# Bf16 pair one-hots, a fused block search and an index fill ahead of the stores in a graph kernel

## The chip, the cores and the metric

The kernel runs on one core of a Trainium2 chip. The metric is the time of one execution on the device in microseconds (us), as the median of several executions.

Five engines run their own instruction streams beside each other and meet at semaphores. TensorE (PE) multiplies matrices into PSUM and loads the weights for it (PEld). VectorE (DVE) and ScalarE (ACT) do elementwise work and reductions. GpSimd (POOL) here issues the indirect DMAs, which gather rows by an index or scatter them. SyncE (SP) issues the plain DMAs.

## The reference

A graph of 6250 nodes with 256 features and 106250 edges (50000 random pairs in both directions and one loop per node, sorted by `dst`) goes through two blocks, each behind a layer normalization and a ReLU, and each added to its input.

```python
h = jnp.maximum(_layernorm(x, axis=-1), 0.0)
# block 0: two hops over the graph
support = h @ weight
h1 = spmm(src, dst, edge_weight, support)      # sum over edges: h1[src] += w * support[dst]
h2 = spmm(src, dst, edge_weight, h1)
x = x + relu(hop_w[0] * h1 + hop_w[1] * h2 + h)
h = jnp.maximum(_layernorm(x, axis=-1), 0.0)
# block 1: neighbour sum and a net of four layers
agg = segment_sum(h[src], dst)
h = (1.0 + eps) * h + agg
h = elu(bn(h @ W1 + b1)); h = elu(bn(h @ W2 + b2)); h = elu(bn(h @ W3 + b3))
x = x + h @ W4 + b4
```

The hops add into `src`, while the edges come sorted by `dst`. So the kernel sorts the edges by `src` itself before it can add them up window by window.

## The kernel before

The kernel is written engine by engine (one function per engine, from line 549 on). The order on each engine is the order of the code, and the engines wait for one another by `wait_ge` on named semaphores. It goes through these stages: normalization, support and bin counts; a rank of every edge in its window; the block search and the sort loop; the sorted edges back into SBUF; hop 1; hop 2 with the second normalization beside it; the neighbour sum with the first layer beside it; the rest of the net.

**Block search.** The edges lie in 832 columns of 128 (`TILES`), which form 16 bins (`BINS`) of 52 columns. A sorted block holds 8 edges of one window (`SLOT`). Each bin has 7 registers of 128 blocks (`REG`). For each bin, register and partition the kernel must find where the block goes in DRAM: it compares 50 start numbers (`NA`) with the block's number, multiplies by the jump at each start and adds up. Before, the starts and the jumps both stand in PSUM (banks 2 and 3, 4 and 5), and the two halves of the bins go one after another: a comparison, a product and a reduction over 8 x 7 x 50 = 2800 elements each (lines 1299 to 1307). `chain` makes the next instruction wait for the one it wraps.

**Sort loop.** The 832 columns go in 64 batches of 13 (`BATCH`, `BATCHES`). In batch k, VectorE makes a one-hot of the slot (13 x 56 elements, line 1323, semaphore `slot_hot`), a one-hot of the partition (13 x 128, line 1328, `part_hot`) and the product of the slot one-hot with the packed edge (line 1332, `load_v`). ScalarE makes the product with the edge weight in 13 activations of 56 columns (line 917, `load_w`). TensorE multiplies the partition one-hot with both products (line 1838, `moved_mm`) and adds up four batches, a bin, in PSUM. All buffers of the loop are double: VectorE's slot one-hot of batch k waits for ScalarE's batch k-2, and the partition one-hot of VectorE and the activations of ScalarE wait for TensorE's batch k-2. After every fourth batch ScalarE copies the bin out of PSUM (`take_bin`, line 908) into one of three buffers, whose earlier bin must have been stored. GpSimd then scatters the bin's 7 registers to DRAM (line 754, `bin_stored`). When all bins are stored, SyncE reads the sorted edges back.

**Hops.** Each hop has 108 groups of 8 columns. Per group ScalarE copies eight index columns into a ring of three (`fill_hop`, line 938, `hop_idx`), GpSimd gathers 8 x 128 rows (`gather`, line 787), VectorE builds one-hots, TensorE multiplies, and VectorE adds. Hop 2 gathers the sums of hop 1, which SyncE stores to `table_hop2` chunk by chunk (`h1_stored`). GpSimd waits for all 13 stores before its first gather of hop 2. Before, ScalarE waits for them too, ahead of its first index copy of hop 2 (lines 967 to 968). Its normalizations in hop 2 write over the sums of hop 1, the first of them in group 16.

**Names.** `w1_all` and `w1_hi_all` are weight buffers that serve as scratch in the sort (`place_i`, `slot_f`). `sum_b` becomes the sums of hop 1 and is scratch before. `work` holds the loop's buffers. `both` gives each such buffer an f32 name, an fp32r name and a bf16 name (`_h`) over the same bytes. `edge_buf` and all that is cut from it (`part_f`, `packed`, `w_all`, the bin numbers) are f32; `iota` is bf16.

Of the kernel before, what the change touches and what calls it, by code (L numbers as in the profile page):

```python
# [43 lines left out]
P = 128  # L44
# [112 lines left out]
def gnn(nc, x, src_t, dst_t, dst_g, w_t, wg, logits, eps, W1, b1, g1, be1, W2, b2, g2, be2,  # L157
        W3, b3, g3, be3, W4, b4, out):
    with ExitStack() as ctx:
# [30 lines left out]
        sum_b, sum_r, sum_h = both("sum_b", DH * ROWS)  # L190
        edge_buf = sb("edge_buf", [P, 4 * TILES + STILES])
        work, work_r, work_h = both("work", 8 * CW)
        w1_all, w1_r, _ = both("w1", K1 * H1)
        w1_sb = w1_all[:, :].rearrange("p (k m) -> p k m", k=K1)
        w4_sb = w1_all[:, :].rearrange("p (k m) -> p k m", k=K4)
        w1_hi_all, w1_hi_sb, w1_hi_h = both("w1_hi", K1 * H1)
# [94 lines left out]
        assert at[0] <= TILES  # L291

        place_i = w1_hi_all[:, 0:TILES].bitcast(I32)
        slot_f = w1_all[:, 0:TILES]
        part_f = dst_loc
        scratch = [sum_b[:, n * TILES:(n + 1) * TILES].bitcast(I32) for n in range(4)]
        at_or_above = sum_b[:, 4 * TILES:4 * TILES + HB * REG * NA].rearrange("p (g r a) -> p g r a", g=HB, a=NA)
        to_block_f = sum_b[:, 4 * TILES + 2 * HB * REG * NA:4 * TILES + 2 * HB * REG * NA + BINS * REG]
        at = [0]
        hot_part = place(2 * BATCH * P).rearrange("p (s t w) -> p s t w", s=2, t=BATCH)  # L300
        hot_slot = place(2 * BATCH * BCOLS).rearrange("p (s t w) -> p s t w", s=2, t=BATCH)
        load = place(2 * BATCH * BCOLS * 2).rearrange("p (s t w v) -> p s t w v", s=2, t=BATCH, v=2)
        ev_bin = place(3 * BCOLS * 2).rearrange("p (s w) -> p s w", s=3)
        to_block = place(BINS * REG).bitcast(I32)
# [77 lines left out]
        def bank(b, n):  # L382

            return ps[:, b, 0:n]
# [44 lines left out]
        spread_mm = sem("spread_mm")  # L429
        rank_mm = sem("rank_mm")  # L430
        rank_picked = sem("rank_picked")
        blocks_placed = sem("blocks_placed")
        places_made = sem("places_made")
        sums_zeroed = sem("sums_zeroed")
# [426 lines left out]
        def _(act):  # L861
# [42 lines left out]
            def take_bin(g):  # L904
# [2 lines left out]
                    act.wait_ge(bin_stored[g % 3], 16 * REG * (g // 3))  # L907
                act.copy(ev_bin[:, g % 3, :], bank(4 + g % 2, 2 * BCOLS)).then_inc(bin_out, 1)

            act.wait_ge(edges_in, 64)  # L910
            act.wait_ge(zeros_stored, 16 * GT)
            for k in range(BATCHES):
# [34 lines left out]
            def hop2_step(i, k, first, last):  # L947
                fill_hop(1, i, k, first)
                c, q = chunk_at(i, k, 5)
                if c is not None:  # L950
                    root(1, c, q, CT)
                c, q = chunk_at(i, k, 7)
                if c is not None:
                    norm(1, c, q, CT)
                c, q = chunk_at(i, k, 8)
                if c is not None:
                    to_cols(c, q, CT)
# [6 lines left out]

            with act.If(near):
                over_hop(act, lambda i, k, first, last: fill_hop(0, i, k, first))
                act.wait_ge(h1_kept, CHUNKS)
                act.wait_ge(h1_stored, 16 * CHUNKS)
                over_hop(act, hop2_step)
                for c in (FULL - 1, FULL):  # L970
                    root(1, c, c % 2, tiles_of(c))
                for c in (FULL - 1, FULL):
                    norm(1, c, c % 2, tiles_of(c))
                for c in (FULL - 1, FULL):
                    to_cols(c, c % 2, tiles_of(c))
# [141 lines left out]
        def _(dve):  # L1117
# [177 lines left out]
            chain(dve.tensor_scalar(scratch[0], place_i, 3, 127, ALU.logical_shift_right, ALU.bitwise_and))  # L1295
            chain(dve.tensor_tensor(scratch[3], scratch[1], scratch[2], ALU.bitwise_or))
            dve.tensor_copy(part_f, scratch[0])
            chain(dve.tensor_copy(slot_f, scratch[3]))
            for half in range(2):
                at_ = [P, HB, REG, NA]  # L1300
                blocks_ = block_no[:, :].unsqueeze(1).unsqueeze(3).to_broadcast(at_)
                start_, jump_ = [bank(b + half, HB * NA).rearrange("p (g a) -> p g a", a=NA).unsqueeze(2).to_broadcast(at_)
                                 for b in (2, 4)]
                chain(dve.tensor_tensor(at_or_above, start_, blocks_, ALU.is_le))
                chain(dve.tensor_tensor(at_or_above, at_or_above, jump_, ALU.mult))
                to = to_block_f[:, half * HB * REG:(half + 1) * HB * REG].rearrange("p (g r) -> p g r", r=REG)
                chain(dve.tensor_reduce(to, at_or_above, AX_X, ALU.add))
            for half in range(2):
# [8 lines left out]
            for k in range(BATCHES):  # L1317
                par = k % 2
                cols = slice(k * BATCH, (k + 1) * BATCH)
                if k >= 2:  # L1320
                    dve.wait_ge(load_w, k - 1)
                at_ = [P, BATCH, BCOLS]
                dve.tensor_tensor(hot_slot[:, par], iota[:, 0:BCOLS].unsqueeze(1).to_broadcast(at_),  # L1323
                                  slot_f[:, cols].unsqueeze(2).to_broadcast(at_), ALU.is_equal).then_inc(slot_hot, 1)
                if k >= 2:
                    dve.wait_ge(moved_mm, k - 1)
                at_ = [P, BATCH, P]
                dve.tensor_tensor(hot_part[:, par], iota[:, 0:P].unsqueeze(1).to_broadcast(at_),
                                  part_f[:, cols].unsqueeze(2).to_broadcast(at_), ALU.is_equal).then_inc(part_hot, 1)
                dve.wait_ge(slot_hot, k + 1)  # L1330
                at_ = [P, BATCH, BCOLS]
                dve.tensor_tensor(load[:, par, :, :, 0], hot_slot[:, par],
                                  packed[:, cols].unsqueeze(2).to_broadcast(at_), ALU.mult).then_inc(load_v, 1)
# [734 lines left out]
```

## Time and profile before

| | |
|---|---|
| median of 3 executions | 4485.47 us (4483.37 to 4486.48) |
| the profiled execution's own time | 4485.46 us |
| its span, first to last instruction | 4483.8 us |
| mean granted TensorE clock | 0.929 |
| busy: TensorE | 3297.6 us (74%) |
| busy: VectorE | 1898.1 us (42%) |
| busy: ScalarE | 796.5 us (18%) |
| busy: GpSimd | 2702.0 us (60%) |

The shares are means over stages with different limits. What is said of one stage must be read from the timeline of that stage. A timeline row gives the start in us from the span's start, the length, the engine and line, what it writes and reads, the number of instructions merged into it, and in brackets the idle time of the engine ahead of it with what ended it. Ends of matmuls are modelled. The line numbers are those of the kernel before.

### The profile page before, as it was taken

How to read it: one execution, taken by the hardware profiler on the slowest of the kernel's cores; microseconds unless marked ns; L12 is line 12 of the kernel's file. 1: busy time of each engine (PE TensorE's matmuls, PEld its weight loads, DVE VectorE, ACT ScalarE, POOL GpSimd, SP SyncE). 2: the span in 40 equal slices, each digit the busy share in tenths (PEclk: the TensorE clock that was granted, in tenths of full speed). 3: DMA queues.
4: the chain of work that ended last, by engine and by line, in shares of the span. 5: the costliest groups of instructions: out<-in, count | busy, mean ns of one | idle time of the engine just before them, and what ended most of it. 6: DMA issues, size and time to landing. Idle time of an engine off the chain costs nothing. (4 is left out here: it accounts for less than half of the span.)

```text
span 4483.8 us, 50632 instructions
## 1 busy us (share of the span) xinstructions
PE 3297.6 (74%) x15959; PEld 2720.9 (61%) x15959; DVE 1898.1 (42%) x4482; ACT 796.5 (18%) x1968; POOL 2702.0 (60%) x2708
## 2 busy tenths in 40 slices
PE   6779577777777767777777774566666665998998
PEld 5278555555555555566655654555555554887887
DVE  7889333333333323333333332222222223556766
ACT  4079100000000000000000000000000001545656
POOL 1088677777777767777777775777777775001000
PEclk9899899999999999999999996888888887999999
DMA  4000233333333343333333344433333333223323
GB/s 141 1 3 6 76 108 109 113 109 109 109 110 112 108 95 109 109 109 112 109 109 109 113 106 120 130 105 105 105 104 104 105 105 92 89 97 125 97 70 115
DMA packets 205561, 443.80 MB, mean 99 GB/s; under 512 B 47053, under 2 KB 121089, under 8 KB 205289
## 3 DMA queue, kind: packets, MB, share of 16 engines
q0 software_dynamic: 126464, 336.63, 26.2%
q1 hardware_dynamic: 78933, 105.26, 7.1%
q8 instruction: 69, 1.13, 0.1%
q14 instruction: 95, 0.78, 0.1%
HBM read 382.22 MB, written 59.49 MB: 99 GB/s over the span
## 5 line engine op out<-in xcount | busy, mean ns | idle before, releaser
L1871 PE MATMUL ps<-work 128*128 128x256 f32 x6912 | 1622.4, 388 | 589.6 <-DMA work<-table_hop,idx 589.6
L787 POOL DMA_INDIRECT work<-table_hop,idx x1728 | 1662.3, 962 | 556.7 <-issue 522.7
L1871 PEld LDWEIGHTS ps<-work 128*128 128x128 f32 x6912 | 1293.2, 192 | 916.9 <-DMA work<-table_hop,idx 491.9
L832 POOL DMA_INDIRECT work<-table_gin,idx x832 | 791.5, 951 | 283.9 <-issue 228.8
L1946 PE MATMUL ps<-work 128*128 128x128 f32 x3328 | 569.5, 342 | 413.9 <-DMA work<-table_gin,idx 382.9
L1946 PEld LDWEIGHTS ps<-work 128*128 128x128 f32 x3328 | 524.7, 248 | 483.6 <-DMA work<-table_gin,idx 314.6
L1409 DVE TENSOR_SCALAR work<-iota,w_hi,edge_buf 128x256 f32<-128x256 bf16 x1728 | 581.4, 408 | 18.4 <-issue 17.3
L938 ACT COPY idx<-w 128x8 int32 (+1 forms) x216 | 42.1, 197 | 1953.9 <-PE ps L1871 1913.3
L1522 DVE TENSOR_TENSOR sum_b<-sum_b,ps 128x256 f32 x104 | 43.9, 422 | 801.0 <-PE ps L1946 801.0
L1421 DVE TENSOR_TENSOR sum_b<-sum_b,ps 128x512 f32 x108 | 74.2, 687 | 721.6 <-PE ps L1871 721.6
L1421 DVE TENSOR_TENSOR big<-big,ps 128x512 f32 x108 | 74.2, 687 | 697.8 <-PE ps L1871 697.8
L1903 PE MATMUL ps<-sum_b_r,work_r 128*128 128x482 f32 (+1 forms) x832 | 318.9, 383 | 35.2 <-DVE sum_b_r L1643 17.9
L1904 PE MATMUL ps<-sum_b_r,work_r 128*128 128x482 f32 (+1 forms) x832 | 318.3, 383 | 0.0
L1905 PE MATMUL ps<-sum_b_r,work_r 128*128 128x482 f32 (+1 forms) x832 | 318.1, 382 | 0.0
L1838 PE MATMUL ps<-work 128*128 128x112 f32 x1664 | 204.4, 281 | 64.9 <-ACT work L917 59.1
L1838 PEld LDWEIGHTS ps<-work 128*128 128x128 f32 x1664 | 195.2, 196 | 74.3 <-issue 74.3
L917 ACT ACTIVATE work<-work,edge_buf 128x56 f32<-128x56 f32 x832 | 200.2, 332 | 151.0 <-DVE work L1323 145.9
L754 POOL DMA_INDIRECT sorted_edges<-work x112 | 197.4, 1762 | 46.8 <-issue 33.2
L819 POOL TENSOR_TENSOR work_r<-work,work_r 128x512 fp32r<-128x512 f32 (+1 forms) x12 | 23.5, 1971 | 326.0 <-DVE work_r L1366 326.0
L1903 PEld LDWEIGHTS ps<-sum_b_r,work_r 128*128 128x128 f32 x832 | 157.3, 189 | 63.0 <-issue 35.6
L985 ACT CAST idx<-edge_buf 128x8 int32 (+1 forms) x104 | 20.2, 198 | 944.5 <-PE ps L1946 944.5
L1509 DVE TENSOR_SCALAR work<-iota,edge_buf 128x128 f32<-128x128 bf16 x832 | 176.2, 299 | 2.0 <-ACT sum_b L944 2.0
(225 smaller groups left out, 2639.7 us busy)
## 6 DMA issues: line engine op xcount, KB each, us to landing
work<-table_hop,idx POOLq DMA_INDIRECT x1728
z_dram<-sum_b SPq DMA_DIRECT2D x24, 964.0 KB, 4.1
sum_b<-z_dram SPq DMA_DIRECT2D x24, 964.0 KB, 5.2
work<-table_gin,idx POOLq DMA_INDIRECT x832
big<-x SPq DMA_DIRECT2D x12, 512.0 KB, 5.9
table_hop<-work SPq DMA_DIRECT2D x12, 512.0 KB, 2.9
table_hop<-sum_b SPq DMA_DIRECT2D x12, 512.0 KB, 3.4
x_dram<-big SPq DMA_DIRECT2D x12, 512.0 KB, 3.4
```

What stands on the lines that cost most here:

```text
L754: pool.indirect_dma_start(sorted_dram, bass.IndirectOffsetOnAxis(to_block[:, g * REG + r:g * REG + r + 1], 0), ev_bin[:, g % 3, r * 2 * SL ...
L787: pool.indirect_dma_start(hop_rows[:, par, t, :], None, table[n], bass.IndirectOffsetOnAxis(idx[:, k % HR, t:t + 1], 0)).then_inc(rows_in[ ...
L832: pool.indirect_dma_start(rows[:, par, t, :], None, table[2], bass.IndirectOffsetOnAxis(idx[:, q, t:t + 1], 0)).then_inc(rows_in[par][half ...
L917: last = act.activation(load[:, k % 2, t, :, 1], hot_slot[:, k % 2, t, :], ACT.Copy, scale=w_all[:, k * BATCH + t:k * BATCH + t + 1])
L1409: last = dve.tensor_scalar(hot[:, k % 2, t, :], iota[:, :], loc_sorted[:, at_], w_sorted[:, at_], ALU.is_equal, ALU.mult)
L1509: last = dve.tensor_scalar(onehot[:, q % 2, t, :], iota[:, 0:WIN], dst_loc[:, bass.ds(g * GT + t, 1)], None, ALU.is_equal)
L1838: mm = pe.matmul(bank(4 + g % 2, 2 * BCOLS), hot_part[:, k % 2, t, :], load[:, k % 2, t].rearrange("p w v -> p (w v)"), start=(r == 0 and ...
L1871: mm = pe.matmul(ps[:, HWIN * par + b, 0:D], hot[:, par, t, b * P:(b + 1) * P], hop_rows[:, par, t, :], start=(t == 0), stop=(t == GT - 1))
L1903: pe.matmul(to[:, 0:n], hi, a[:, 0, 0:n], start=start, stop=False)
L1904: pe.matmul(to[:, 0:n], hi, a[:, 1, 0:n], start=False, stop=False)
L1905: return pe.matmul(to[:, 0:n], lo, a[:, 0, 0:n], start=False, stop=stop)
L1946: mm = pe.matmul(ps[:, 2 * par + a, 0:WIN], rows[:, par, t, a * P:(a + 1) * P], onehot[:, par, t, :], start=(t == 0), stop=(t == GT - 1))
```

## The change

The slot number of an edge was an f32 number per column (`slot_f`). It is now a bf16 number that is written twice side by side (`slot_twice`), and the slot one-hot `hot_slot` is bf16 and made over pairs: its innermost dimension is two neighbouring columns, which meet the two copies of the slot number. ScalarE's and VectorE's products read the bf16 one-hot and still write f32. The partition one-hot is unchanged.

In the block search, ScalarE copies both start tables from PSUM to SBUF (`starts_of`, new semaphore `starts_kept`) as soon as the ranks are picked. VectorE then runs one fused operation per half and register (compare with the register's block number, times the jump), 7 of 400 elements a half, in place of the comparison and the product of 2800. The reduction stays.

In hop 2, ScalarE's wait for the stores of hop 1 moves from the first index copy to the first normalization.

```diff
@@ -190,7 +190,7 @@
         sum_b, sum_r, sum_h = both("sum_b", DH * ROWS)
         edge_buf = sb("edge_buf", [P, 4 * TILES + STILES])
         work, work_r, work_h = both("work", 8 * CW)
-        w1_all, w1_r, _ = both("w1", K1 * H1)
+        w1_all, w1_r, w1_h = both("w1", K1 * H1)
         w1_sb = w1_all[:, :].rearrange("p (k m) -> p k m", k=K1)
         w4_sb = w1_all[:, :].rearrange("p (k m) -> p k m", k=K4)
         w1_hi_all, w1_hi_sb, w1_hi_h = both("w1_hi", K1 * H1)
@@ -291,14 +291,18 @@
         assert at[0] <= TILES
 
         place_i = w1_hi_all[:, 0:TILES].bitcast(I32)
-        slot_f = w1_all[:, 0:TILES]
+        slot_twice = w1_h[:, 0:2 * TILES].rearrange("p (t u) -> p t u", u=2)
         part_f = dst_loc
         scratch = [sum_b[:, n * TILES:(n + 1) * TILES].bitcast(I32) for n in range(4)]
         at_or_above = sum_b[:, 4 * TILES:4 * TILES + HB * REG * NA].rearrange("p (g r a) -> p g r a", g=HB, a=NA)
         to_block_f = sum_b[:, 4 * TILES + 2 * HB * REG * NA:4 * TILES + 2 * HB * REG * NA + BINS * REG]
+        at = [4 * TILES + 2 * HB * REG * NA + BINS * REG]
+        starts_of = sum_b[:, at[0]:at[0] + BINS * NA].rearrange("p (g a) -> p g a", a=NA)
+        assert at[0] + BINS * NA <= DH * ROWS
         at = [0]
         hot_part = place(2 * BATCH * P).rearrange("p (s t w) -> p s t w", s=2, t=BATCH)
-        hot_slot = place(2 * BATCH * BCOLS).rearrange("p (s t w) -> p s t w", s=2, t=BATCH)
+        hot_slot = work_h[:, 2 * at[0]:2 * at[0] + 2 * BATCH * BCOLS].rearrange("p (s t w) -> p s t w", s=2, t=BATCH)
+        place(2 * BATCH * BCOLS)
         load = place(2 * BATCH * BCOLS * 2).rearrange("p (s t w v) -> p s t w v", s=2, t=BATCH, v=2)
         ev_bin = place(3 * BCOLS * 2).rearrange("p (s w) -> p s w", s=3)
         to_block = place(BINS * REG).bitcast(I32)
@@ -429,6 +433,7 @@
         spread_mm = sem("spread_mm")
         rank_mm = sem("rank_mm")
         rank_picked = sem("rank_picked")
+        starts_kept = sem("starts_kept")
         blocks_placed = sem("blocks_placed")
         places_made = sem("places_made")
         sums_zeroed = sem("sums_zeroed")
@@ -907,6 +912,11 @@
                     act.wait_ge(bin_stored[g % 3], 16 * REG * (g // 3))
                 act.copy(ev_bin[:, g % 3, :], bank(4 + g % 2, 2 * BCOLS)).then_inc(bin_out, 1)
 
+            act.wait_ge(rank_picked, 2 * BT)
+            act.wait_ge(spread_mm, 4)
+            act.copy(starts_of.rearrange("p (h g) a -> p h (g a)", h=2), ps[:, 2:4, 0:HB * NA]).then_inc(starts_kept, 1)
+
+
             act.wait_ge(edges_in, 64)
             act.wait_ge(zeros_stored, 16 * GT)
             for k in range(BATCHES):
@@ -950,6 +960,9 @@
                 if c is not None:
                     root(1, c, q, CT)
                 c, q = chunk_at(i, k, 7)
+                if first and c is not None:
+                    act.wait_ge(h1_kept, CHUNKS)
+                    act.wait_ge(h1_stored, 16 * CHUNKS)
                 if c is not None:
                     norm(1, c, q, CT)
                 c, q = chunk_at(i, k, 8)
@@ -964,8 +977,6 @@
 
             with act.If(near):
                 over_hop(act, lambda i, k, first, last: fill_hop(0, i, k, first))
-                act.wait_ge(h1_kept, CHUNKS)
-                act.wait_ge(h1_stored, 16 * CHUNKS)
                 over_hop(act, hop2_step)
                 for c in (FULL - 1, FULL):
                     root(1, c, c % 2, tiles_of(c))
@@ -1295,14 +1306,16 @@
             chain(dve.tensor_scalar(scratch[0], place_i, 3, 127, ALU.logical_shift_right, ALU.bitwise_and))
             chain(dve.tensor_tensor(scratch[3], scratch[1], scratch[2], ALU.bitwise_or))
             dve.tensor_copy(part_f, scratch[0])
-            chain(dve.tensor_copy(slot_f, scratch[3]))
+            chain(dve.tensor_copy(slot_twice, scratch[3].unsqueeze(2).to_broadcast([P, TILES, 2])))
             for half in range(2):
-                at_ = [P, HB, REG, NA]
-                blocks_ = block_no[:, :].unsqueeze(1).unsqueeze(3).to_broadcast(at_)
-                start_, jump_ = [bank(b + half, HB * NA).rearrange("p (g a) -> p g a", a=NA).unsqueeze(2).to_broadcast(at_)
-                                 for b in (2, 4)]
-                chain(dve.tensor_tensor(at_or_above, start_, blocks_, ALU.is_le))
-                chain(dve.tensor_tensor(at_or_above, at_or_above, jump_, ALU.mult))
+                start_ = starts_of[:, half * HB:(half + 1) * HB, :]
+                jump_ = bank(4 + half, HB * NA).rearrange("p (g a) -> p g a", a=NA)
+                if half == 0:
+                    dve.wait_ge(starts_kept, 1)
+                for r in range(REG):
+                    last = dve.scalar_tensor_tensor(out=at_or_above[:, :, r, :], in0=start_, scalar=block_no[:, r:r + 1],
+                                                    in1=jump_, op0=ALU.is_le, op1=ALU.mult)
+                chain(last)
                 to = to_block_f[:, half * HB * REG:(half + 1) * HB * REG].rearrange("p (g r) -> p g r", r=REG)
                 chain(dve.tensor_reduce(to, at_or_above, AX_X, ALU.add))
             for half in range(2):
@@ -1319,9 +1332,10 @@
                 cols = slice(k * BATCH, (k + 1) * BATCH)
                 if k >= 2:
                     dve.wait_ge(load_w, k - 1)
-                at_ = [P, BATCH, BCOLS]
-                dve.tensor_tensor(hot_slot[:, par], iota[:, 0:BCOLS].unsqueeze(1).to_broadcast(at_),
-                                  slot_f[:, cols].unsqueeze(2).to_broadcast(at_), ALU.is_equal).then_inc(slot_hot, 1)
+                at_ = [P, BATCH, BCOLS // 2, 2]
+                columns = iota[:, 0:BCOLS].rearrange("p (w u) -> p w u", u=2).unsqueeze(1).to_broadcast(at_)
+                dve.tensor_tensor(hot_slot[:, par].rearrange("p t (w u) -> p t w u", u=2), columns,
+                                  slot_twice[:, cols, :].unsqueeze(2).to_broadcast(at_), ALU.is_equal).then_inc(slot_hot, 1)
                 if k >= 2:
                     dve.wait_ge(moved_mm, k - 1)
                 at_ = [P, BATCH, P]
```

On VectorE, around the block search, the last cast, the first half and the first batch stand like this before (`sum_b` holds the search's scratch, `w` the slot numbers, `work` the one-hots; `dve_small` is the semaphore of `chain`):

```order
L1298 CAST w<-sum_b 128x832
L1304 TENSOR_TENSOR sum_b<-ps,block_no 128x2800 [waits dve_small]
L1305 TENSOR_TENSOR sum_b<-sum_b,ps 128x2800 [waits dve_small]
L1307 TENSOR_REDUCE sum_b<-sum_b 128x56 [waits dve_small]
...
L1311 TENSOR_TENSOR work<-sum_b,block_no 128x56 [waits dve_small]
...
L1314 MEMSET done 128x1
L1323 TENSOR_TENSOR work<-iota,w 128x728
L1328 TENSOR_TENSOR work<-iota,edge_buf 128x1664
L1332 TENSOR_TENSOR work<-work,edge_buf 128x728 [waits slot_hot]
```

and like this after the change:

```order
L1309 CAST w_h<-sum_b 128x1664
L1316 SCALAR_TENSOR_TENSOR sum_b<-sum_b,block_no,ps 128x8x50 [waits starts_kept,dve_small]
L1316 SCALAR_TENSOR_TENSOR sum_b<-sum_b,block_no,ps 128x8x50 x6
L1320 TENSOR_REDUCE sum_b<-sum_b 128x56 [waits dve_small]
...
L1324 TENSOR_TENSOR work<-sum_b,block_no 128x56 [waits dve_small]
...
L1327 MEMSET done 128x1
L1337 TENSOR_TENSOR work_h<-iota,w_h 128x728
L1342 TENSOR_TENSOR work<-iota,edge_buf 128x1664
L1346 TENSOR_TENSOR work<-work_h,edge_buf 128x728 [waits slot_hot]
```

Two operations over 2800 elements became seven over 8 x 50, the first of which waits for ScalarE's copy. The cast writes 1664 elements in place of 832. The loop has the same three instructions in the same order, the first of them now into bf16.

On ScalarE, where hop 2 begins, the index copies (`idx<-w`) and the first normalization (`lsd<-lve`, `sum_b<-big,lnm,lrs`) stand like this before:

```order
L938 COPY idx<-w 128x8 [waits sorted_ready,hop_mm] x18
L938 COPY idx<-w 128x8 [waits hop_mm,sorted_ready,h1_stored,h1_kept]
L938 COPY idx<-w 128x8 [waits sorted_ready,hop_mm] x14
L868 ACTIVATE lsd<-lve 128x4 [waits ln1_var]
L938 COPY idx<-w 128x8 [waits sorted_ready,hop_mm] x2
L876 ACTIVATE sum_b<-big,lnm,lrs 128x256 [waits ln1_coef]
```

and after:

```order
L948 COPY idx<-w 128x8 [waits sorted_ready,hop_mm] x33
L873 ACTIVATE lsd<-lve 128x4 [waits ln1_var]
L948 COPY idx<-w 128x8 [waits sorted_ready,hop_mm] x2
L881 ACTIVATE sum_b<-big,lnm,lrs 128x256 [waits ln1_coef,h1_stored,h1_kept]
L881 ACTIVATE sum_b<-big,lnm,lrs 128x256 x3
L948 COPY idx<-w 128x8 [waits sorted_ready,hop_mm]
```

The first 18 copies of the first piece are the last of hop 1. The waits for `h1_stored` and `h1_kept` moved from the first copy of hop 2 to the first normalization, 16 groups on.

## Rows read from the trace of the kernel before

**Rows 1.** Busy time by stretch of the sort loop; then clock, DMA share, GB/s

```profile
217.60:299.13 81.53, 55.82 (x442) 53.45 (x442) 65.83 (x59) 56.90 (x239) 67.53 (x12) 0.86 0.01 2
299.13:462.92 163.79, 148.57 (x1222) 141.77 (x1222) 155.72 (x135) 145.29 (x609) 133.24 (x95) 0.99 0.03 6
```

**Rows 2.** Timeline, VectorE, search and first batch (start, us, what, idle before)

```profile
194.24 0.59 DVE L1292 TENSOR_SCALAR w_hi<-w 128x832 int32<-128x832 f32 x1
...
198.07 0.58 DVE L1298 CAST w<-sum_b 128x832 f32<-128x832 int32 x1
198.69 3.08 DVE L1304 TENSOR_TENSOR sum_b<-ps,block_no 128x2800 f32<-128x2800 f32 x1
201.80 3.07 DVE L1305 TENSOR_TENSOR sum_b<-sum_b,ps 128x2800 f32<-128x2800 f32 x1
...
217.60 0.91 DVE L1323 TENSOR_TENSOR work<-iota,w 128x728 f32<-128x728 bf16 x1
...
218.43 1.88 DVE L1328 TENSOR_TENSOR work<-iota,edge_buf 128x1664 f32<-128x1664 bf16 x1
220.23 0.91 DVE L1332 TENSOR_TENSOR work<-work,edge_buf 128x728 f32<-128x728 f32 x1
221.05 0.91 DVE L1323 TENSOR_TENSOR work<-iota,w 128x728 f32<-128x728 bf16 x1
```

**Rows 3.** Groups by line of VectorE, shapes apart (busy us, mean ns, idle before)

```profile
L1638 DVE SCALAR_TENSOR_TENSOR edge_buf<-edge_buf 128x482 f32<-128x482 f32 x144 | 94.6, 657 | 55.0 <-PE ps L1905 38.9 <-ACT edge_buf L1036 16.1
...
L1170 DVE TENSOR_TENSOR sum_b_h<-iota,edge_buf 128x784 bf16<-128x784 bf16 x32 | 29.4, 967 | 0.0
```

**Rows 4.** Timeline, ScalarE, two batches of the loop and its end

```profile
248.76 3.13 ACT L917 ACTIVATE work<-work,edge_buf 128x56 f32<-128x56 f32 x13 [0.33 <-DVE work L1323]
251.79 0.23 ACT L908 COPY work<-ps 128x112 f32<-128x112 f32 x1
252.21 3.13 ACT L917 ACTIVATE work<-work,edge_buf 128x56 f32<-128x56 f32 x13 [0.19 <-DVE work L1323]
...
462.92 0.25 ACT L908 COPY work<-ps 128x112 f32<-128x112 f32 x1 [3.31 <-PE ps L1838]
481.82 1.71 ACT L928 COPY edge_buf<-ps 128x432 f32<-128x432 f32 x2 [18.64 <-PE ps L1847]
```

**Rows 5.** Timeline, TensorE, one batch and the last

```profile
255.49 3.13 PE L1838 MATMUL ps<-work 128*128 128x112 f32 x26 [0.22 <-ACT work L917]
...
459.76 3.13 PE L1838 MATMUL ps<-work 128*128 128x112 f32 x26 [0.32 <-ACT work L917]
```

**Rows 6.** Waits of the loop (us in total, times, longest us)

```profile
ACT work L908 <- DMA sorted_edges<-work: 16.3, 1, 16.3
...
DVE work L1323 <- ACT work L917: 13.2, 1, 13.2
DVE work L1328 <- PE ps L1838: 6.7, 2, 4.2
```

**Rows 7.** Timeline, GpSimd, scatters of the sorted blocks

```profile
239.10 47.87 POOL L754 DMA_INDIRECT sorted_edges<-work  x1 [10.80 <-ACT work L908]
287.27 0.97 POOL L754 DMA_INDIRECT sorted_edges<-work  x1 [0.31 <-issue]
...
308.98 1.49 POOL L754 DMA_INDIRECT sorted_edges<-work  x1 [0.30 <-issue]
```

**Rows 8.** Timeline, VectorE, beside those scatters

```profile
285.01 0.91 DVE L1332 TENSOR_TENSOR work<-work,edge_buf 128x728 f32<-128x728 f32 x1
...
309.55 0.91 DVE L1332 TENSOR_TENSOR work<-work,edge_buf 128x728 f32<-128x728 f32 x1
```

**Rows 9.** Timeline, ScalarE and GpSimd, hop 1 to hop 2

```profile
1595.98 0.39 ACT L938 COPY idx<-w 128x8 int32<-128x8 int32 x3 [39.90 <-DMA table_hop<-sum_b]
1597.01 1.19 POOL L787 DMA_INDIRECT work<-table_hop,idx  x1 [16.48 <-ACT idx L938]
```


## The prediction

> **What bounds the kernel now.** I read the page first for the shares, then the busy time by stretch, then the timeline of each engine inside the sort, the waits of that stretch, and last the timeline where hop 1 passes into hop 2. The change touches three places: the block search, the loop of 64 batches that moves the edges into their slots, and the hand-over between the hops. Everything behind the first gather of hop 1 is the same program and only starts earlier, so I price the three places and shift the rest.
>
> In the loop VectorE is the busiest engine in both stretches, 65.83 of 81.53 us and 155.72 of 163.79 us [rows 1]. In the timeline it runs one batch after another without a gap: the slot one-hot (L1323) starts at 217.60, the partition one-hot (L1328) 0.83 us later, the product (L1332) 1.80 us after that, and the next batch's slot one-hot 0.82 us after that [rows 2]. That is 3.45 us a batch and 221 us for 64. From 217.60 to the end of TensorE's last batch at 459.76 + 3.13 = 462.89 [rows 5] are 245.3 us. The difference is 6.7 us of VectorE waiting for TensorE, 13.2 us of VectorE waiting for ScalarE [rows 6], and a tail of about 4 us in which TensorE finishes. The other engines are close behind. ScalarE starts its bin copy 3.03 us after the first of its 13 activations [rows 4], and TensorE's batch takes 3.13 us [rows 5]. So the question of the prediction is where the loop stops following VectorE.
>
> **Block search.** Before, each half runs a comparison and a product of 2800 elements and a reduction of as many. The first one starts at 198.69, the first batch at 217.60 [rows 2]: 18.9 us with VectorE alone at work. The product starts 3.11 us behind the comparison, and the three of a half are 3 x 3.11 = 9.3 us. After, the two tensor operations of a half become seven fused ones of 400 elements. The nearest row is the same operation at 482 elements, 657 ns [rows 3]. The 728-element one-hot lasts 0.91 us and is followed after 0.83 us [rows 2], so an element costs 1.04 ns and a further operation in a row 0.07 us. That gives 400 x 1.04 + 70 = 0.49 us, seven of them 3.4 us, and 0.1 us for the chain's wait behind the last. A half is then 3.5 + 3.1 = 6.6 us and both save 2 x (9.3 - 6.6) = 5.4 us. The reduction stays. If the overhead of an operation did not overlap at all (0.15 us in place of 0.07), 14 x 0.08 = 1.1 us of it would be lost.
>
> The fused operations take one start table from SBUF, which ScalarE must copy first (800 columns). Its wait ends when the ranks are picked, at 194.24 [rows 2]; the nearest copies are two of 432 columns in 1.71 us together [rows 4]. VectorE gets to the search only at 198.69, so 4.4 us cover at most 1.7. Nothing that is due stands behind it on ScalarE, whose next work needs the first slot one-hot. I cost it at nothing, and at 1.7 us without that cover. The cast of the slot numbers now writes each twice: 832 elements took 0.58 us [rows 2], which is two elements a cycle. Twice as many at that rate is +0.43 us, at one element a cycle +1.7 - 0.4 = +1.3 us. I take 0.4, since the row is of this very operation. The place before the loop therefore gives 5.4 - 0.4 = 5.0 us, between 2.9 and 5.4.
>
> **The slot one-hot in the loop.** Its output, its iota and its slot numbers are now all bf16, and the innermost dimension is a pair that is read in steps of one. No row shows a two-tensor operation with 16-bit operands alone. At the slow end nothing changes: the bin one-hots, which already write bf16 but read an f32 number per element, take 967 ns for 784 [rows 3], one element a cycle like L1323. At the fast end stands the cast of 832 in 0.58 us [rows 2]: at two elements a cycle 728 end after 728/2 x 1.04 + 150 = 0.53 us, with the next following after 0.45. I take 0.45 us, because the cast shows that the engine can write two a cycle and because both slow rows have a 32-bit operand, which the new one no longer has.
>
> The Trainium skill (VectorE: DVE Perf Modes, section "Mode 2×_1P — pack two bf16 into one 32-bit read") states that an operation on two tensors makes two results a cycle if its operands are 16-bit and step by one. By that rule the slot one-hot takes 0.45 us and the partition one-hot, whose second operand stays f32, keeps its 1.80. The slow rows agree with it; no row shows its fast side.
>
> VectorE's batch would then be 0.45 + 1.80 + 0.82 = 3.07 us. But the loop doesn't get there. ScalarE's batch k+2 writes the load buffer that TensorE reads in batch k, so it waits for that batch. ScalarE's batch takes 3.13 us to the end of its last activation, TensorE starts 0.15 us later (252.21 + 3.13 = 255.34 against 255.49) and takes 3.13 us [rows 4, 5], and its end releases the next engine 0.03 us later (462.89 against 462.92). Two batches per round: (3.13 + 0.15 + 3.13 + 0.03) / 2 = 3.22 us. Every fourth batch the bin copy, some 0.2 us, stands in the same wait: 3.27 us. I take 3.25, a saving of 0.20 us a batch. In about four batches, two at each restart, TensorE sets the pace already. 60 x 0.20 = 12.0 us. This round leaves VectorE a gap of 3.25 - 3.07 = 0.18 us in front of the partition one-hot. The product (f32, one per cycle) stays at 0.82, and ScalarE's activations, which now read bf16, are taken at their old length, the only row there is; 0.02 us more on each of 13 would eat the whole saving.
>
> I leave the big pause in the loop as it is. GpSimd's first scatter starts at 239.10 and takes 47.87 us [rows 7]. It ends 1 us after VectorE falls silent at 285.01 + 0.91 = 285.92 [rows 8], because ScalarE waits 16.3 us for that bin to be stored [rows 6]. What starts earlier by the saving also stops earlier by it. The seven scatters behind the last batch are unchanged.
>
> **Hop 2's indices.** ScalarE's first copy starts at 1595.98, when the last table store has landed, and GpSimd's first gather at 1597.01 [rows 9]. The copies now stand ready, and GpSimd, which has a wait for the same stores of its own, no longer waits for the 0.2 us of the copy and its signal. Most of the 1.03 us stays as GpSimd's start, which in the trace follows ScalarE's copy, not the store: I take 0.3 us, with 0 and 1.0 as ends. The wait on the stores now sits before the first normalization, 16 groups later, when they have long landed, and costs nothing.
>
> **Sum.** 5.0 + 12.0 + 0.3 = 17.3 us. The profiled execution took 4485.46 us (span 4483.8 and 1.7 around it), as good as the median of 4485.47, so I forecast 4468 us.
>
> **Rivals.**
> - *VectorE goes on setting the pace.* If TensorE's ends, which are modelled, come earlier than shown, the loop runs at 3.07 us: 60 x 0.38 = 23 us and 4457 us. For it speaks that the round is only 0.15 us longer than VectorE's batch; against it the 0.03 us from TensorE's end to its waiters, which leaves little to be early. 0.13.
> - *The pause goes.* With a gap in each batch the first scatter may finish beside VectorE. Then 13.2 us and the 4.2 us of the restart behind it [rows 6] go as well: 17 us more, 4451 us. For it: the scatter ended as soon as VectorE was silent. Against it: later scatters got through without a gap, so what the first one lacks isn't known. 0.09.
> - *The one-hot stays at one element a cycle.* Then only the search and the hand-over count: 5.3 us, 4480 us. 0.12.
> - *GpSimd falls behind, and the kernel gets slower.* Beside VectorE a scatter waits for an instruction to end: the one begun at 308.98 ends 0.92 us after VectorE's next instruction starts at 309.55 [rows 7, 8], and the next begins 0.30 us later. So two pass per batch, where a bin needs 7 in 4 batches. From the product's start to the next partition one-hot are now 0.82 + 0.45 = 1.27 us, and the next scatter begins 0.92 + 0.30 = 1.22 us after that start: 0.05 us of margin. A scatter that nothing holds lasts 0.97 us, 0.05 more than those 0.92, so it asks about 0.05 us behind its start and no margin is left. If it misses and no gap helps it, one passes per batch: four beside a bin's four batches (12.3 us), three more at 1.27 us (0.97 and 0.30, [rows 7]) with VectorE silent, and up to 4.2 us of restart, 16.1 to 20.3 us a bin in place of 13.8. Over 13 bins that is +30 to +84 us, less 5.3: 4510 to 4564 us. It decides from under 1.75 scatters a batch. Against it stands the 0.18 us gap, in which the scatter gets through. 0.06.
>
> The Trainium skill (SBUF — State Buffer, section "Who interferes with whom") states that a VectorE instruction with two SBUF inputs shuts out a GpSimd instruction that reads SBUF, and the later one is blocked until the other ends. The trace agrees: 0.97 us alone, 1.49 us beside VectorE [rows 7]. By that rule shorter VectorE instructions alone would do GpSimd no harm.
>
> **Numbers.** The forecast has 0.58, with its own range of 4461 to 4476 us (3.15 to 3.35 us a batch, with the ends of the other two terms); 0.02 is left for what I have not thought of. A measurement here tells 0.2%, 9 us, from no change. All of the forecast but a sliver, the first two rivals and none of the third are faster: 0.79. Same is 0.14, slower 0.07. The range from 4450 to 4480 us holds the first three cases and about half of the third rival.
>
> **What would show it.** After, the slot one-hot should last about 0.53 us in the timeline, VectorE should wait for TensorE before each partition one-hot, and batches should follow at 3.2 to 3.3 us. Fourteen fused operations should start 0.49 us apart, and the search should end 13.3 us after it starts. The first scatter should again end as VectorE falls silent. A slot one-hot at 0.91 us, activations longer than 0.33 us, or scatters of 3 us would make the forecast wrong.

## The result and the profile after

The changed kernel takes **4445.87 us** (median of four executions, 4445.09 to 4447.0) where the kernel before took 4485.74. The ratio is 0.9912, 95% interval 0.9895 to 0.9929. That is 39.9 us less, where 17.3 were forecast, and 4 us below the range's lower end. The profiled executions have spans of 4444.7 and 4483.8 us.

Busy time by stretch of the changed kernel (the columns of [rows 1]): search, sort loop, and the way from the loop's end to the first gather of hop 1.

```profile
195.08:214.27 19.19, 0.00 (x0) 0.00 (x0) 18.91 (x26) 0.82 (x1) 0.00 (x0) 0.61 0.00 0
214.27:429.84 215.57, 202.10 (x1664) 192.84 (x1664) 201.62 (x194) 201.63 (x847) 163.91 (x106) 0.98 0.03 5
429.84:452.32 22.48, 3.15 (x16) 2.82 (x16) 5.46 (x10) 2.35 (x6) 7.15 (x7) 0.61 0.13 42
```

Before, the search ran from 194.24 to 217.60 [rows 2], 23.36 us, and the loop from there to 462.92, 245.32 us [rows 1]. So the search gives 4.2 us and the loop 29.7, where 5.0 and 12.0 were forecast. The search itself began 0.8 us later (195.08 against 194.24). Some 5 us more come from the two hops: counted from its first gather to the first gather of the next stage, hop 1 took 1109.0 us in place of 1111.6, and hop 2 1118.1 in place of 1120.9.

VectorE's timeline, search and first batch of the changed kernel:

```profile
198.91 1.02 DVE L1309 CAST w_h<-sum_b 128x1664 bf16<-128x1664 int32 x1
199.96 3.88 DVE L1316 SCALAR_TENSOR_TENSOR sum_b<-sum_b,block_no,ps 128x400 f32<-128x400 f32 x7
203.87 3.07 DVE L1320 TENSOR_REDUCE sum_b<-sum_b 128x56 f32<-128x2800 f32 x1
206.98 3.88 DVE L1316 SCALAR_TENSOR_TENSOR sum_b<-sum_b,block_no,ps 128x400 f32<-128x400 f32 x7
...
214.27 0.53 DVE L1337 TENSOR_TENSOR work_h<-iota,w_h 128x728 bf16<-128x728 bf16 x1
...
214.72 1.88 DVE L1342 TENSOR_TENSOR work<-iota,edge_buf 128x1664 f32<-128x1664 bf16 x1
```

The slot one-hot lasts 0.53 us and the next operation follows after 0.45, as forecast; before it was 0.91 and 0.83 [rows 2]. The cast took 1.02 us in place of 0.58: +0.44. Seven fused operations take 3.88 us, 0.55 each.

ScalarE's bin copies in the changed loop, four batches apart, and VectorE beside them at the same pace:

```profile
246.53 0.25 ACT L913 COPY work<-ps 128x112 f32<-128x112 f32 x1
...
259.61 0.25 ACT L913 COPY work<-ps 128x112 f32<-128x112 f32 x1
```

```profile
233.42 1.89 DVE L1342 TENSOR_TENSOR work<-iota,edge_buf 128x1664 f32<-128x1664 bf16 x1
235.23 0.91 DVE L1346 TENSOR_TENSOR work<-work_h,edge_buf 128x728 f32<-128x728 bf16 x1
236.06 0.53 DVE L1337 TENSOR_TENSOR work_h<-iota,w_h 128x728 bf16<-128x728 bf16 x1
236.89 1.89 DVE L1342 TENSOR_TENSOR work<-iota,edge_buf 128x1664 f32<-128x1664 bf16 x1 [0.30 <-PE ps L1852]
```

13.08 us for four batches are 3.27 us each: the round of ScalarE and TensorE. VectorE waits for TensorE (0.30 us here) in front of about every second partition one-hot. What the forecast missed stands on GpSimd, in its timeline and in the waits of the loop:

```profile
234.58 1.78 POOL L759 DMA_INDIRECT sorted_edges<-work  x1 [9.60 <-ACT work L913]
236.67 0.97 POOL L759 DMA_INDIRECT sorted_edges<-work  x1 [0.31 <-issue]
237.95 1.67 POOL L759 DMA_INDIRECT sorted_edges<-work  x1 [0.30 <-issue]
...
247.06 2.21 POOL L759 DMA_INDIRECT sorted_edges<-work  x1 [0.94 <-ACT work L913]
```

```profile
POOL sorted_edges L759 <- ACT work L913: 24.6, 16, 9.6
...
DVE work L1342 <- PE ps L1852: 9.9, 30, 2.8
ACT work L927 <- PE ps L1852: 9.6, 31, 2.8
```

The first scatter takes 1.78 us, not 47.87 [rows 7]. The 16.3 us in which ScalarE waited for a stored bin and the 13.2 us in which VectorE waited for ScalarE [rows 6] are gone. Instead there are some thirty short waits for TensorE. GpSimd keeps up: it waits 0.94 us for the second bin.

That first scatter ended at 234.58 + 1.78 = 236.36. VectorE ran without idle time from 233.42 on and first fell idle behind the slot one-hot of 236.06, until 236.89. So here the scatter was through before the gap came.

One of hop 1's last blocks, its last table stores and the first gather of hop 2, on TensorE, the DMA queue and GpSimd (the stores of the kernel before stand first):

```profile
1591.99 1.15 SPq L586 DMA_DIRECT2D table_hop<-sum_b  x2
```

```profile
1545.71 3.69 PE L1885 MATMUL ps<-work 128*128 128x256 f32 x16 [3.33 <-DMA work<-table_hop,idx]
...
1556.56 1.15 SPq L591 DMA_DIRECT2D table_hop<-sum_b  x2
...
1561.31 1.14 POOL L792 DMA_INDIRECT work<-table_hop,idx  x1 [15.46 <-DMA table_hop<-sum_b]
```

GpSimd now waits for the stores themselves and no longer for ScalarE's copy [rows 9]. From the last stores' issue to that gather it is 4.75 us in place of 5.02.

### The profile page after: what moved, and what is told of

The parts are those of the page before. It is cut to its first block and busy times, and to the rows that moved or that the text cites. A ratio compares the mean times of both kernels' runs of the same rounds, so it can differ in the third digit from the quotient of the medians.

```text
span 4444.7 us, 50645 instructions
## 1 busy us (share of the span) xinstructions
PE 3284.7 (74%) x15959; PEld 2715.9 (61%) x15959; DVE 1873.4 (42%) x4492; ACT 797.2 (18%) x1969; POOL 2662.6 (60%) x2708
## 5 line engine op out<-in xcount | busy, mean ns | idle before, releaser
L927 ACT ACTIVATE work<-work_h,edge_buf 128x56 f32<-128x56 bf16 x832 | 199.9, 333 | 29.0 <-DVE work_h L1337 19.0
L759 POOL DMA_INDIRECT sorted_edges<-work x112 | 160.5, 1433 | 53.9 <-issue 29.2
```

The costliest lines, as they stand in the source:

```text
L759: pool.indirect_dma_start(sorted_dram, bass.IndirectOffsetOnAxis(to_block[:, g * REG + r:g * REG + r + 1], 0), ev_bin[:, g % 3, r * 2 * SL ...
L927: last = act.activation(load[:, k % 2, t, :, 1], hot_slot[:, k % 2, t, :], ACT.Copy, scale=w_all[:, k * BATCH + t:k * BATCH + t + 1])
```

## The experiments

Three theories at the start. G: the long scatter is a matter of VectorE's gaps; the faster one-hot leaves VectorE idle for a moment, and that lets the first scatter in. Its rivals: L (luck), the pause went only because the loop began some 3 us earlier against the other engines; O, the pause hangs on the 16-bit operands or on the amount of VectorE's work.

**Part 1 alone** (the kernel before with the changed slot one-hot, its cast and its buffers, and nothing else).

> Only the paired bf16 slot one-hot; the search and the index copies as before. Both theories hold the loop at 3.27 us a batch (209 us for 64). Theory G (VectorE's new idle slots, or its shorter first instruction, let the first scatter through): the first scatter takes about 2 us, the loop 215 to 216 us in place of 245, the total about 4451 to 4457 us. Theory L (luck: the pause went only because the loop began 3 us earlier against the other engines): the first scatter still takes some 40 us, the loop 230 us, the total 4466 to 4473 us.

4455.39 us against 4484.62, ratio 0.9938 (0.9921 to 0.9954). The first scatter of its GpSimd timeline:

```profile
238.47 1.79 POOL L759 DMA_INDIRECT sorted_edges<-work  x1 [9.15 <-ACT work L913]
```

The one-hot alone takes the pause away, in a loop that begins at 218.61, not earlier than before. L falls.

**Parts 2 and 3 alone** (the changed kernel with the slot one-hot of before).

> Only the block search and the index copies; the slot one-hot stays f32, so VectorE runs without a gap at 3.45 us a batch. Theory G: the pause stays (first scatter some 48 us, loop 245 us), the total is 4480 to 4482 us. Theory L: the pause goes, loop 228 us, total 4463 us. The search should gain 4.6 us by either, the hand-over of the hops 0.3 us.

4478.71 us against 4484.62, ratio 0.9989 (0.9979 to 0.9999). The loop begins at 214.90, 2.7 us earlier than before, and the pause is there:

```profile
236.36 47.86 POOL L758 DMA_INDIRECT sorted_edges<-work  x1 [10.75 <-ACT work L912]
```

**The changed kernel with VectorE's gap filled.** One more operation per batch, whose result nobody reads (part of the diff; the semaphore `filled` is new).

```diff
+                if k > 0:
+                    dve.wait_ge(filled, k)
+                dve.tensor_tensor(w1_all[:, TILES:TILES + 192], w_all[:, 0:192], packed[:, 0:192],
+                                  ALU.mult).then_inc(filled, 1)
                 if k >= 2:
                     dve.wait_ge(moved_mm, k - 1)
```

> The changed kernel, with one more VectorE instruction of 192 elements (about 0.27 us) per batch behind the slot one-hot, whose result nothing reads. VectorE's batch is then 3.34 us and it has no idle slot. Theory G in its narrow form (the idle slot is what the first scatter needs): the pause comes back, first scatter some 40 us, loop about 234 us, total 4463 to 4467 us. Theory O (the kind of the one-hot's operands, bf16 throughout, is what lets the scatter in): first scatter about 2 us, loop 219 us, total 4449 to 4451 us.

4471.56 us, ratio 0.997 (0.9958 to 0.9983): above the expected 4463 to 4467. VectorE's batch is 3.35 us, as counted. Some 3 us of the excess are in the loop, which took 450.89 - 213.61 = 237.3 us where 234 were expected, and the rest is behind it; neither is explained. The 16-bit operands are still there, the gap is not, and the pause is back. GpSimd, and VectorE where that scatter begins:

```profile
233.40 46.51 POOL L760 DMA_INDIRECT sorted_edges<-work  x1 [9.08 <-ACT work L914]
```

```profile
232.65 1.88 DVE L1347 TENSOR_TENSOR work<-iota,edge_buf 128x1664 f32<-128x1664 bf16 x1
```

The filling moved something else too. The scatter now begins 0.75 us into a partition one-hot; in the changed kernel it began 1.16 us into one (234.58 against 233.42), and in the kernel before 0.83. So this run does not tell the missing gap from the other place.

**The kernel before with four idle slots.** VectorE waits for its own partition one-hot before the product (part of the diff).

```diff
                 dve.wait_ge(slot_hot, k + 1)
+                if 5 <= k < 9:
+                    dve.wait_ge(part_hot, k + 1)
```

> The kernel before, where in batches 5 to 8 alone VectorE waits for its own partition one-hot to be finished before it starts the product: four idle slots of about 0.1 us, 0.4 us in all. The first scatter starts in batch 6. Theory G: a slot of 0.1 us suffices, the first scatter takes about 2 us, the pause of 17 us goes, total 4468 to 4470 us. Theory O, or a first scatter that is slow by itself: nothing changes, 4485 to 4487 us.

4468.44 us against 4484.62, ratio 0.9964 (0.995 to 0.9978). VectorE's timeline shows the first slot as 0.10 us between 239.51 + 1.88 and 241.50; GpSimd's shows the scatter beside it:

```profile
239.51 1.88 DVE L1328 TENSOR_TENSOR work<-iota,edge_buf 128x1664 f32<-128x1664 bf16 x1
241.50 0.92 DVE L1334 TENSOR_TENSOR work<-work,edge_buf 128x728 f32<-128x728 f32 x1
```

```profile
240.34 2.11 POOL L754 DMA_INDIRECT sorted_edges<-work  x1 [10.20 <-ACT work L908]
...
268.18 2.52 POOL L754 DMA_INDIRECT sorted_edges<-work  x1 [2.74 <-ACT work L908]
```

No instruction is faster in this kernel: 0.4 us of added idle time save 16 us. The scatter begins 0.83 us into a partition one-hot, as in the kernel before, so the place is the same and the idle slot alone differs. O falls, and an idle slot is enough to let a scatter in. That a gap is also what lets it in in the changed kernel does not follow: there it ended 0.2 us before VectorE was idle. GpSimd's spans are rough in the profile, but the traces of all four runs with the changed one-hot and no filling show the same 1.78 or 1.79 us. A rival stands: the scatter may have got in for its place, 1.16 us into the partition one-hot. A run with that place and no gaps in VectorE was not made.

**One idle slot** (`if k == 5` in place of the four batches) asks whether the others follow by themselves.

> The kernel before with the idle slot of some 0.1 us in batch 5 alone. Theory F (once a scatter has got in, the others follow at the boundaries of VectorE's instructions): as with four slots, first scatter some 2.1 us, 4467 to 4471 us. Theory S (each scatter needs an idle slot of its own): the first passes in some 2.1 us, a scatter right behind it takes over 40 us, and the time is 4482 to 4486 us.

4472.27 us against 4492.53 on that chip, ratio 0.9957 (0.9941 to 0.9972). One slot is enough. GpSimd, and VectorE's first and ScalarE's last row of the loop:

```profile
239.07 2.11 POOL L754 DMA_INDIRECT sorted_edges<-work  x1 [9.99 <-ACT work L908]
241.49 1.34 POOL L754 DMA_INDIRECT sorted_edges<-work  x1 [0.31 <-issue]
...
252.46 2.53 POOL L754 DMA_INDIRECT sorted_edges<-work  x1 [0.93 <-ACT work L908]
```

```profile
218.37 0.91 DVE L1323 TENSOR_TENSOR work<-iota,w 128x728 f32<-128x728 bf16 x1
```

```profile
445.44 0.25 ACT L908 COPY work<-ps 128x112 f32<-128x112 f32 x1 [3.31 <-PE ps L1840]
```

**An early scatter** (one to unread dump rows during the rank stage) asks whether it is only the program's first.

> The kernel before, with one indirect scatter more: GpSimd writes 128 rows into the dump rows that nobody reads, during the rank stage, and waits for its end; the sort loop is untouched, VectorE has no idle slot in it. Theory F (only the first scatter of the program needs the idle slot, whatever it then has to set up): the first scatter of the loop takes 1.5 to 2.5 us, the 16.3 and 13.2 us waits go, and the time is 4467 to 4471 us. Theory S (any scatter that begins beside a VectorE without gaps is shut out, wherever it stands in the program): the first scatter of the loop still takes 46 to 48 us, and the time is 4484 to 4488 us.

4480.63 us against 4492.53, ratio 0.9975 (0.9964 to 0.9985), between the two expectations; the trace decides. The loop's first scatter is still shut out, so being the program's first is not what matters. The loop takes 463.67 - 218.47 = 245.2 us, as before. The gain stands in the two hops, which together take 11.3 us less than in the run with one idle slot on the same chip (2708.14 - 486.17 us against 2701.26 - 467.95, from hop 1's first gather to the first behind hop 2). Why is not explained.

```profile
239.18 47.75 POOL L762 DMA_INDIRECT sorted_edges<-work  x1 [9.93 <-ACT work L916]
```

**The filled kernel with four idle slots** (both diffs above).

> e3_filled (the changed kernel with one operation more per batch, so that VectorE has no gap; 4471.6 us), and in batches 5 to 8 VectorE waits for its own partition one-hot, four idle slots of some 0.1 us. Theory G (an idle slot lets the first scatter in, and the pause was what cost e3_filled its time beside the operation itself): first scatter 1.5 to 2.5 us, 4452 to 4456 us. Theory O (the pause comes from the amount of VectorE's work, not from its gaps): 4470 to 4473 us.

4461.23, 4464.35, 4476.05 and 4481.17 us: neither theory's number. The profiled execution, the 4481.17 one, shows why:

```profile
235.39 2.18 POOL L760 DMA_INDIRECT sorted_edges<-work  x1 [9.11 <-ACT work L914]
...
262.30 46.94 POOL L760 DMA_INDIRECT sorted_edges<-work  x1 [2.80 <-ACT work L914]
```

The first scatter got in at the slots, where without them (the filled kernel above, the same 0.75 us into a partition one-hot) it was shut out. But the first one of the third bin, 2.80 us after the one ahead and with VectorE without gaps again, was shut out in turn. Whether the two faster executions escaped that was not recorded.

**A later scatter made late** (one idle slot, and the third bin's first scatter waits for a product):

```diff
                 pool.wait_ge(bin_out, g + 1)
+                if g == 2:
+                    pool.wait_ge(load_v, 14)
```

> e8_one_idle (the kernel before with one idle slot of VectorE in batch 5), and GpSimd waits for the product of batch 13 before the first scatter of the third bin, so that this scatter comes some 4 us after the last one instead of 0.9 us, beside a VectorE without gaps. Theory H (a scatter is shut out where GpSimd has been without one for some us before it; e7_filled_idle's 46.94 us one came 2.8 us after the scatter ahead): that scatter takes over 30 us, ScalarE waits for a free bin buffer and the time is 15 to 18 us above e8_one_idle's, some 0.9995 of the kernel before. Theory F (once the first scatter is in, none is shut out): 1.3 to 2.6 us, and e8_one_idle's ratio of 0.9957 again.

4485.27 us against 4484.22, ratio 1.0002 (0.9993 to 1.0011). The whole gain of the idle slot is gone again, by a delay of some 3 us on an engine with time to spare:

```profile
253.06 2.53 POOL L756 DMA_INDIRECT sorted_edges<-work  x1 [0.93 <-ACT work L910]
...
270.15 45.01 POOL L756 DMA_INDIRECT sorted_edges<-work  x1 [4.20 <-DVE work L1336]
```

So theory F falls: a later bin's scatter can be shut out too. Two more runs ask what decides it, with the same wait on `slot_hot` and on `part_hot`:

> e9_later_bin with another event: the first scatter of the third bin waits for the slot one-hot of batch 13, so that it comes some 1.5 us after the scatter ahead and begins about 0.8 us into a partition one-hot, where the kernel before began the one of 47.87 us. Theory H (what counts is how long GpSimd has been without a scatter; 0.93 and 2.74 us were let in, 2.80 and 4.20 us were not): 1.3 to 2.6 us, and a time some 15 us under the kernel before. Theory P (what counts is where in VectorE's instruction it begins): over 30 us, and the time of the kernel before.

> e9_later_bin with another event: the first scatter of the third bin waits for the partition one-hot of batch 13, so that it comes some 3.3 us after the scatter ahead and begins in a product, not in a partition one-hot, in which all scatters that were shut out so far have begun. Theory H (the length of the gap decides, and it lies above 2.80 us): over 30 us, and the time of the kernel before. Theory P (the place in VectorE's instruction decides): 1.3 to 2.6 us, some 15 us less than the kernel before.

The short gap gave 4463.29 us beside 4484.31, one execution of each, and the scatter was let in:

```profile
267.50 1.88 POOL L756 DMA_INDIRECT sorted_edges<-work  x1 [1.57 <-DVE work L1325]
```

It began 0.85 us into a partition one-hot (266.65 in its VectorE timeline), where the kernel before began the one of 47.87 us. So P, the place alone, falls. The other one had a mean granted clock of 0.805, the kernel before 0.929 (so its 4533.19 us are not compared), but its scatter answers: let in, 3.37 us behind the last, at the start of a slot one-hot. GpSimd's and VectorE's timelines:

```profile
280.97 0.96 POOL L756 DMA_INDIRECT sorted_edges<-work  x1 [3.37 <-DVE work L1330]
```

```profile
280.13 0.91 DVE L1336 TENSOR_TENSOR work<-work,edge_buf 128x728 f32<-128x728 f32 x1
280.96 0.96 DVE L1325 TENSOR_TENSOR work<-iota,w 128x728 f32<-128x728 bf16 x1
```

So H, the length of the gap alone, falls too. Every scatter seen shut out came 2.80 us or more after the last one and began in a partition one-hot, 0.01 to 0.83 us behind its start. The two together are not enough: the changed kernel's first scatter came after 9.60 us, began 1.16 us into a partition one-hot and got in with VectorE busy throughout. That the place counts for a scatter that comes late would fit all rows; it is not shown.

**What the 5 us behind the loop are.** Part 3 undone, and the changed kernel once more.

> The changed kernel with its third part undone: hop 2's indices are filled only after the stores of the layer's output. Theory A (the third part is worth what the hand-over between the hops shows, 5.02 to 4.75 us, and the last blocks of the hops are something else): 4445.0 to 4447.5 us. Rival B (filling ahead also spares the some 5 us that the changed kernel has less behind the sort loop): 4450 to 4452 us.

> The changed kernel again, with nothing altered, to see how much of its gain stays from execution to execution. Theory A (34 us come from the sort and its loop and are the same each time, the some 5 us behind it are the hops' last blocks and vary): the loop ends within 1 us of 429.84, ratio 0.991 to 0.993. Rival B (the 5 us belong to the change): ratio 0.9905 to 0.9915, and the last blocks of the hops take 3.7 us as in the first trace.

Without part 3: 4455.65 us (4447.11 to 4459.85) against 4492.53, ratio 0.992 (0.9906 to 0.9933): not to be told from the changed kernel's. The changed kernel again: 4450.52 against 4484.22, ratio 0.9925 (0.9911 to 0.9939), with its loop from 214.72 to 429.75, 215.0 us beside 215.6. So 34 us came back, and 6 did not; the two intervals overlap, and these 6 us are not clear of noise. Its TensorE timeline has slow blocks near the ends of both hops, where the first trace had none:

```profile
1538.62 5.41 PE L1885 MATMUL ps<-work 128*128 128x256 f32 x16 [2.34 <-DMA work<-table_hop,idx]
1545.84 3.69 PE L1885 MATMUL ps<-work 128*128 128x256 f32 x16 [1.81 <-DMA work<-table_hop,idx]
...
2656.97 10.12 PE L1885 MATMUL ps<-work 128*128 128x256 f32 x32 [3.24 <-DMA work<-table_hop,idx]
```

Hop 1 took 1109.3 us all the same, 0.3 more than in the first trace, and hop 2 1120.1, 2.0 more. The ratio lies in theory A's range, and the loop came back as A says; rival B's 0.9905 to 0.9915 is not excluded by the interval. What makes the last blocks slow in one execution and not in another stays open.

## Why the prediction was wrong

**The step that failed** is "I leave the big pause in the loop as it is", a term put at nothing. The pause went, and with it 18 us. The kernel before with one idle slot has a loop of 445.44 - 218.37 = 227.1 us instead of 245.3: the pause is worth 18.2 us. That leaves 11.5 us of the loop's 29.7 for the one-hot's own share, by difference; 60 batches of 3.45 - 3.27 us would give 10.8. The rival "The pause goes" named what happened (the first scatter finishes beside VectorE) and, at 4451 us, all but 5 us of the time; it got 0.09. Its reason, a gap in each batch, is borne out in part: an idle slot put beside a shut-out scatter frees it, but the changed kernel's own trace has the scatter through before the gap. I had computed the gap of 0.18 us myself, and had used it against the rival in which GpSimd falls behind. I had the row that spoke for the rival: the scatter ended when VectorE fell silent. Against it I set that later scatters pass without a gap. They do, by [rows 7, 8], but those follow one another in 0.30 us, and the one in question came after 10.80 us of waiting. So they said little of a scatter that comes after a long wait. With the cause unknown I still reasoned: "What starts earlier by the saving also stops earlier by it."

**What held.** The slot one-hot at two elements a cycle: 0.53 and 0.45 us to the digit, so the third rival is out. The round of ScalarE and TensorE: 3.27 us a batch was worked out for it with the bin copy (I took 3.25), and the saving came out at 11.5 us against 12.0, by the difference above. So VectorE does not set the pace, and the first rival is out. ScalarE's activations on bf16 kept their length (3.12 us for 13 where it was 3.13). The copy of the start table (0.82 us, 4.9 us ahead of its use) cost nothing, and the cast +0.44. GpSimd did not fall behind. The wait for TensorE stood in front of about every second partition one-hot, not of each (30 in 64 batches).

**What was mis-sized.** A fused operation follows the last after 0.55 us, not 0.49: the 0.07 us that I put on top of each came from operands in SBUF, and here one stands in PSUM (that this is why was not tested). 14 x 0.06 = 0.8 us, and the search gave 4.2 instead of 5.0. The hand-over between the hops went from 5.02 to 4.75 us, by 0.3 as forecast. The hops' some 5 us of the first trace were not in the forecast; the second measurement of the changed kernel gained 6 us less, which its interval does not tell from noise.

## What to carry to other kernels

A transfer that one engine must issue can hang on a pause of another that has nothing to do with it: before you leave a long instruction "as it is", ask what ended it, and whether the change makes that come sooner. An engine without any gap is not a virtue in itself; here 0.1 us of idle time, put into the kernel before on the loop's busiest engine, was worth some 18 us. Test such a cause from both sides, by taking the gap away from the fast kernel and giving it to the slow one. Then see in the fast kernel's own timeline whether the event falls into the gap: here it did not, and a cure that works is not yet the cause.

## What was not expected of the hardware

An indirect scatter on GpSimd beside a VectorE that runs tensor_tensor operations back to back can be held for 45 to 48 us, over 37 to 53 starts of VectorE instructions, until VectorE falls silent; one slot of 0.1 us frees it (2.11 us). The runs here measured 47.87, 47.86, 46.51, 47.75, 46.94 and 45.01 us for it. It is not bound to happen: the changed kernel's first scatter took 1.78 us beside such operations, with no idle time of VectorE in it. The Trainium skill (SBUF — State Buffer, section "Who interferes with whom") says that a VectorE instruction with two SBUF inputs contends with a GpSimd instruction that reads SBUF, and that the order of issue decides which of the two blocks. The scatters of 1.3 to 2.5 us in the loop agree with a wait for one instruction: they end about 0.92 us behind the start of VectorE's next one. The six long ones do not: they lost at every boundary between two VectorE instructions. Of two scatters that began 0.01 us behind an instruction's start, one was let in (280.97, 0.96 us, and that slot one-hot took 0.96 instead of 0.91) and one shut out (270.15, behind the partition one-hot of 270.14).
